# Expert weights in two halves with separate release, two of the four early pairs behind the rows' write, and row turns moved next to the raw turns

## What is computed

```python
def _L0_ffn_ref(x, Wg, bg, Wge, bge, W1, b1, W2, b2):
    G, E = (4, 8); KG, KE = (2, 2); D, M = (192, 768)
    xf = x.reshape(-1, D)
    comb = _combine_weights(xf, Wg, bg, Wge, bge)      # two groups of four, two experts in each: 4 of 32
    h = gelu(einsum('nd,edm->nem', xf, W1) + b1, approximate=False)
    y = einsum('nem,emd->ned', h, W2) + b2
    return einsum('ne,ned->nd', comb, y).reshape(x.shape)

h = tokens(x)                                   # (8, 64, 192)
h = h + _L0_attn_ref(_layernorm(h), ...)        # the first attention
h = h + _L0_ffn_ref(_layernorm(h), ...)         # the 32 experts
h = h + _L1_attn_ref(_layernorm(h), ...)        # the second attention
h = h + _L1_ffn_ref(_layernorm(h), ...)
```

## Time and profile before

| | us |
|---|---|
| median of 3 runs | 325.53 |
| the three runs | 325.77, 325.53, 323.02 |
| the profiled execution | 324.14 |
| its span, first to last instruction | 322.3 |
| PE busy | 290.0 |
| DVE busy | 152.6 |
| ACT busy | 112.4 |
| POOL busy | 64.6 |

### The profile page before, as it was taken

One profiled execution on the slowest core, in us unless ns is written; L12 is line 12 of the kernel. 1 busy time (PEld: TensorE's weight loads), 2 busy tenths in 40 slices (PEclk: granted clock), 3 DMA queues, 4 the chain that ended last, 5 costly groups with the idle time before them and its releaser, 6 DMA issues.

```text
span 322.3 us, 7312 instructions
## 1 busy us (share of the span) xinstructions
PE 290.0 (90%) x2642; PEld 194.5 (60%) x2642; DVE 152.6 (47%) x431; ACT 112.4 (35%) x386; POOL 64.6 (20%) x76
## 2 busy tenths in 40 slices
PE   7899699798999999998999999995689899969994
PEld 6858687573666565554565565553657687445553
DVE  0664335736365354434444542320159566554554
ACT  1256015203234535434435435434034464511110
POOL 4500000050223334333333233112034000000000
PEclk9999659959799999999999999999599999999999
DMA  7999402010299999999999999903840000000001
GB/s 276 395 421 420 176 2 65 1 47 13 53 411 418 407 411 416 416 413 421 411 416 417 412 414 415 395 26 126 321 206 1 4 2 2 0 0 0 0 2 49
DMA packets 13044, 70.91 MB, mean 220 GB/s; under 512 B 2849, under 2 KB 4070, under 8 KB 6736
## 3 DMA queue, kind: packets, MB, share of 16 engines
q1 hardware_dynamic: 10416, 65.62, 50.5%
q0 software_dynamic: 2304, 3.68, 3.4%
q10 hardware_dynamic: 288, 1.13, 0.9%
HBM read 68.97 MB, written 3.28 MB: 224 GB/s over the span
## 4 chain that ended last, share of the span: by engine, by line
PE 64%; DMA 19%; DVE 9%; issue 3%; ACT 2%; SPq 2%; DVEq 0%; ACTq 0%; POOLq 0%
PE ps L975 11%; PE ps L928 7%; DMA late_in<-in_experts 7%; PE ps L747 4%; DMA expert_w<-in_experts 4%; PE ps L933 4%; DMA probs<-in_experts 4%; PE ps L1050 4%; PE ps L1038 4%; PE ps L947 3%; PE ps L669 3%; DMA attn_rows<-in_attn_rows 2%; PE ps L1005 2%; PE ps L1041 2%; PE ps L918 2%
## 5 line engine op out<-in xcount | busy, mean ns | idle before, releaser
L637 ACT ACTIVATE turned<-ps,route_in 128x64 f32<-128x64 f32 x288 | 61.4, 340 | 83.4 <-PE ps L947 83.4
L484 POOL DMA_INDIRECT x_rows<-xn_rows,row_ids x24 | 24.9, 1038 | 117.5 <-DVE row_ids L1245 116.6
L1259 DVE COPY probs<-ps 128x768 f32<-128x768 f32 x24 | 23.0, 957 | 40.9 <-PE ps L933 40.9
L496 POOL DMA_INDIRECT y_picks<-fexp,row_ids x24 | 24.9, 1038 | 40.8 <-DVE fexp L1344 40.8
L975 PE MATMUL ps<-expert_w,turned 128*64 128x192 f32 x288 | 27.7, 345 | 0.0
L975 PE MATMUL ps<-late_in,turned 128*64 128x192 f32 x216 | 26.2, 331 | 1.2 <-ACT turned L637 1.2
L1344 DVE COPY fexp<-ps 128x192 f32<-128x192 f32 x24 | 8.6, 357 | 31.7 <-PE ps L975 31.7
L975 PEld LDWEIGHTS ps<-expert_w,turned 128*64 128x64 f32 x288 | 20.6, 143 | 4.6 <-issue 1.8
L975 PEld LDWEIGHTS ps<-late_in,turned 128*64 128x64 f32 x216 | 19.1, 137 | 6.3 <-ACT turned L637 2.4
L947 PE MATMUL ps<-cst,probs 128*128 128x128 f32 x144 | 21.1, 281 | 0.9 <-DVE probs L1259 0.9
L928 PE MATMUL ps<-expert_w,fexp 128*64 128x384 f32 x96 | 18.1, 498 | 2.8 <-DMA expert_w<-in_experts 2.0
(11 more groups left out here) (240 smaller groups left out, 460.1 us busy)
## 6 DMA issues: line engine op xcount, KB each, us to landing
expert_w<-in_experts SPq DMA_DIRECT2D x24, 1152.0 KB, 10.5
late_in<-in_experts SPq DMA_DIRECT2D x18, 1152.0 KB, 9.0
probs<-in_experts SPq DMA_DIRECT2D x6, 1152.0 KB, 11.5
late_in<-in_ffn_in SPq DMA_DIRECT2D x1, 2592.0 KB, 12.7
probsT<-in_patches SPq DMA_DIRECT2D x4, 384.0 KB, 7.0
qk_padT<-y_picks SPq DMA_DIRECT2D x4, 384.0 KB, 4.7
late_in<-in_attn_in SPq DMA_DIRECT2D x1, 864.0 KB, 4.3
attn_w<-in_attn_w SPq DMA_DIRECT2D x1, 673.5 KB, 9.0
```

The source lines that it names most:

```text
L484: pool.indirect_dma_start(out=x_rows[:, x_u, :], out_offset=None, in_=xn_rows, in_offset=bass.IndirectOffsetOnAxis(ap=row_ids[:, u % STEPS ...
L496: pool.indirect_dma_start(out=y_picks, out_offset=bass.IndirectOffsetOnAxis(ap=row_ids[:, u, 1:2], axis=0), in_=y_rows[:, u % RING, :], in ...
L637: last = act.activation(hidden[:, u % 2, half * (KH // 2) + c, slots_of(q)], ps[:, 4 + half, c * P + q * SLOTS:c * P + (q + 1) * SLOTS], A ...
L1259: dve.tensor_copy(raw.rearrange("p (h n) -> p h n", h=2), ps[:, 2:4, 0:HID // 2]).then_inc(raw_sb, 1)
```

## The change

Four things change.

1. Each expert comes in two transfers, W1 (columns 0 to 1151) and W2 (the rest), each with a semaphore of its own for each slot (`w1_dma`, `w2_dma`). The up matmuls wait for the first, the down matmuls for the second. The W1 half of pair `u + 5` is loaded when the up matmuls of pass `u + 1` are done, the W2 half of pair `u + 4` when the down matmuls of pass `u` are.
2. Of the four early pairs, 0 and 1 are loaded where they were, and 2 and 3 behind the write of `xn_rows`.
3. The row turns are done for `u + 3` behind the raw turns, at the end of the loop body, and VectorE copies them out behind the output copy. The 14 matmuls that make tables for the later passes go behind the first down matmuls.
4. Of the five fillers of 256 columns ahead of pass 0 one is left.

The diff, cut to its core:

```diff
-            def load_pair(i, ov_round, u):
+            def load_pair(i, ov_round, u, cols, done):
                 for q in range(PAIR):
                     e = expert_of(sp, i, ov_round, u, q)
-                    sp.dma_start(weights[u % RING * PAIR + q], dram["experts"][bass.ds(e, 1), :, :].rearrange("a p n -> (a p) n")).then_inc(w_dma[u % RING], 16)
-
-            for u in range(RING):
-                load_pair(0, None, u)
+                    sp.dma_start(weights[u % RING * PAIR + q][:, cols], dram["experts"][bass.ds(e, 1), :, cols].rearrange("a p n -> (a p) n")).then_inc(done[u % RING], 16)
+            def load_first(i, ov_round, u):
+                load_pair(i, ov_round, u, slice(0, W1_COLS), w1_dma)
+            def load_second(i, ov_round, u):
+                load_pair(i, ov_round, u, slice(W1_COLS, W_COLS), w2_dma)
+            for u in range(RING // 2):
+                load_first(0, None, u)
+                load_second(0, None, u)
             sp.wait_ge(xn_ready, 2 * NT)
             ...
+            for u in range(RING // 2, RING):
+                load_first(0, None, u)
+                load_second(0, None, u)
+            sp.wait_ge(up_mm, 1)
+            load_first(0, None, RING)
             def feed(i, ov_round, first, tiles):
                 for u in range(STEPS):
                     with where_tile(sp, tiles, ov_round, u):
+                        with where_tile(sp, tiles, ov_round, u + 1 + RING):
+                            sp.wait_ge(up_mm, i * STEPS + u + 2)
+                            load_first(i, ov_round, u + 1 + RING)
                         with where_tile(sp, tiles, ov_round, u + RING):
                             sp.wait_ge(down_mm, i * STEPS + u + 1)
-                            load_pair(i, ov_round, u + RING)
+                            load_second(i, ov_round, u + RING)
...
# TensorE, ids_in
+                if not (isinstance(tile, int) and tile < IDS_AHEAD):
+                    pe.wait_ge(rowsT_sb, tile - 1)
# TensorE, up_in
-                pe.wait_ge(w_dma[u % RING], 16 * PAIR * (i * (STEPS // RING) + u // RING + 1))
+                pe.wait_ge(w1_dma[u % RING], 16 * PAIR * (i * (STEPS // RING) + u // RING + 1))
# TensorE, experts
-                        with where_tile(pe, tiles, ov_round, u + 2):
-                            rows_in(i, u + 2)
...
+                        pe.wait_ge(w2_dma[u % RING], 16 * PAIR * (i * (STEPS // RING) + u // RING + 1))
...
                         with where_tile(pe, tiles, ov_round, u + 1):
                             turn_raw(i, u + 1, first)
+                        with where_tile(pe, tiles, ov_round, u + 3):
+                            rows_in(i, u + 3)
# TensorE, ahead of pass 0
-            keep_busy(5, 5)
+            keep_busy(1, 5)
...
             turn_raw(0, 0)
+            rows_in(0, 2)
# VectorE, results
-                        with where_tile(dve, tiles, ov_round, u + 2):
-                            dve.wait_ge(rowsT_mm, i * STEPS + u + 3)
-                            with where_tile(dve, tiles, ov_round, u + IDS_AHEAD):
-                                ids_out(i, u + IDS_AHEAD, first)
-                            rows_out(u)
+                        with where_tile(dve, tiles, ov_round, u + IDS_AHEAD):
+                            ids_out(i, u + IDS_AHEAD, first)
...
                         dve.tensor_copy(y_rows[:, u % RING, :], ps[:, 6 + u % 2, 0:D]).then_inc(y_ready, 1)
+                        with where_tile(dve, tiles, ov_round, u + 3):
+                            dve.wait_ge(rowsT_mm, i * STEPS + u + 4)
+                            rows_out(u + 3)
```

More of the change, by code:

```diff
@@ L348, in vit_tower @@
         pick_diag_ready, picks_mm = sem("pick_diag_ready"), sem("picks_mm")
-        w_dma, x_dma, y_dma = ([sem(f"{n}{u}") for u in range(RING)] for n in ("w_dma", "x_dma", "y_dma"))
+        w1_dma, w2_dma, x_dma, y_dma = ([sem(f"{n}{u}") for u in range(RING)] for n in ("w1_dma", "w2_dma", "x_dma", "y_dma"))
         rowsT_mm, rowsT_sb, up_mm, raw_sb, rawT_mm, gelu_done, down_mm, y_ready = (
@@ L957, in experts @@
                             ids_in(i, u + IDS_AHEAD, ov_round)
-                        with where_tile(pe, tiles, ov_round, u + 2):
-                            rows_in(i, u + 2)
                         if first and u == 0:
                             pe.wait_ge(ov_onehot_ready, 1)
-                            for c in range(KH):
-                                nc.tensor.matmul(ps[:, 7, 256 + c * NOV:256 + (c + 1) * NOV], b1_rows[:, c * P:(c + 1) * P], ov_onehot[:, :], start=True, stop=True)
-                            nc.tensor.matmul(ps[0:1, 7, 256 + KH * NOV:256 + (KH + 1) * NOV], const("row", NE), ov_onehot[:, :], start=True, stop=True).then_inc(ov_mm, 1)
                         if first and u == 1:
@@ L977, in experts @@
                         last.then_inc(down_mm, 1)
+                        if first and u == 0:
+                            for c in range(KH):
+                                nc.tensor.matmul(ps[:, 7, 256 + c * NOV:256 + (c + 1) * NOV], b1_rows[:, c * P:(c + 1) * P], ov_onehot[:, :], start=True, stop=True)
+                            nc.tensor.matmul(ps[0:1, 7, 256 + KH * NOV:256 + (KH + 1) * NOV], const("row", NE), ov_onehot[:, :], start=True, stop=True).then_inc(ov_mm, 1)
                         with where_tile(pe, tiles, ov_round, u + 1):
                             turn_raw(i, u + 1, first)
+                        with where_tile(pe, tiles, ov_round, u + 3):
+                            rows_in(i, u + 3)
             pe.wait_ge(tables_ready, 2)
@@ L1283, in _ @@
                                      op0=ALU.is_lt, op1=ALU.mult).then_inc(ov_onehot_ready, 1)
+            dve.wait_ge(rowsT_mm, 3)
+            rows_out(2)
             def ov_places():
```

## The result

| | before | after |
|---|---|---|
| median of the runs | 325.65 (323.02 to 328.97, 4 runs) | 309.04 (308.32 to 311.46, 4 runs) |
| the profiled execution, its span | 324.14, 322.3 | 308.32, 306.5 |
| mean granted clock | 0.951 | 0.953 |

A forecast was written before the change was run, and what follows sets the result against it. Bounds: a stall and half clock in the first attention, fillers before the passes, TensorE and then weights in them. Terms of -1.9, -3.0, -3.0, -1.1 and 0 took 324.14 to 315.1 us, 316.5 as a median; range 310.5 to 322.

The forecast's parts named there:

- A: First attention: early pairs 2 and 3 behind the rows' write remove TensorE's stall; -1.9 us, bounds 0 and 2.43.
- B: First attention, behind the stall: the half clock on the matmuls goes; -3.0 us, bounds 0 and 5.1.
- C: Expert passes: split pairs, W1 released by the up matmuls, end waits for weights; -3.0 us, bounds 0 and 3.0.
- D: Expert passes: row turns next to the raw turns cost 0.10 us less a pass; -1.1 us, at most 2.2.
- Rival 1: First attention: the stall stays, and the half clock with it; 321.4 us, chance 0.28.
- E: Start of the passes: four fillers fewer, earlier row turns against a possible half clock; 0 us, bounds -1.7 and +2.3.
- rival 3: Expert passes: row turns wait for gathers in a ring through VectorE; slower, up to 329.5 us, chance 0.04.
- Rival 2: Expert passes: split transfers bring nothing, weights stay 6.05 us a pass; 319.5 us, chance 0.14.
- Rival 4: Late passes: VectorE's wait for row turns loses the lead on weights; about 1 us, no chance of its own.

## Why the prediction was wrong

The direction held and each mechanism is there, but the sum was 7.6 us short by the medians. Against the profiled execution it was 6.8 short (15.8 for 9.0): 3.6 of it in A and B, 3.1 in C and D, 2.0 at the start of the passes, and 1.9 the other way at the end. Two steps failed. B, the largest shortfall, was sized at 3.0 for a half clock that costs 5.2 to 5.6 us, above even its bound of 5.1. C and D were costed one by one, C against a wrong length of the pass, and they are worth more together. By its steps:

**A, the stall (forecast -1.9).** Held. The issue piece of 2.16 to 2.43 us is in all six profiles with four pairs at the front, and is at most 0.79 long in the seven others that have no pause put in. The kernel with one pair behind the write shows that it takes load in that very stretch. In the writes' column, a stall without a dip costs 47.9 - 45.2 = 2.8 us (47.87 and 48.01, against the mean of the six profiles with at most 0.23 of stall), somewhat more than the piece and than my bound of 2.43. Rival 1, the stall as a matter of the instructions alone, is out. That the stalled engine was short of instructions can be read off the DMA view. Every profile has one instruction transfer of 16 KB shortly ahead of this place: it starts at 32.29 to 33.01 us in the six with four pairs at the front (in that of before, the transfer of the earlier trace rows, at 32.42), and at 29.58 to 31.22 in the eight others. After, in 29 to 31 us:

```profile
q8 instruction: 1, 0.02, 3.0%
```

In all nine profiles in which TensorE stands still behind the 117th small matmul, it goes on 2.35 to 2.73 us after the start of this transfer, also in the three with a short stall (0.22 us, transfer at 31.19; 0.23, at 30.54; 0.79, at 31.22). In the five in which the transfer starts 2.8 us or more ahead of the end of that matmul, there is no stall. The transfer itself takes 1.07 to 1.08 us under load and 0.93 to 1.33 without: what the load delays is its start. The Trainium skill, "Runtime: NRT & Kernel Launch" (Instruction fetch mechanics), has the fetch mostly hidden by the running block; these traces agree while the DMA engines rest, but for the 0.79 us, and show it bare at 410 GB/s.

**B, the half clock (forecast -3.0 of at most 5.1).** A failed step, mis-sized. With a dip the write leaves at 51.86 to 53.70, without one, behind the same stall, at 47.9: 5.2 us on the mean, 5.6 in this pair of traces. I took 3.0 because the dip might only come later. It did not: the stretch stays at 1.00 to its end. The bound of 5.1 was short because it began at the weighing: the 27 small matmuls ahead of it take 1.11 us at half clock before, and 0.68 in the kernel with one filler, which has the stall and no dip. A and B together are -8.51 for -4.9. What I had not seen is that the dip is a matter of chance. In the profiles it comes behind four of the six stalls and never without one, and the pause alone gives two groups of runs. That points to idleness of TensorE as what opens the way to it, and not to load, since in the pause the DMA engines move 4 GB/s; a trace of the slower group would be needed to show it. It fits with the spread: all runs of the kernel before lie from 316.28 to 329.44 us, and the fastest have the highest mean clock (0.977 at 316.28 and 316.63, 0.935 to 0.955 for those above 323), while the four runs of after spread over 3.1. From the fastest of before to the fastest of after (308.32) it is 8.0 us. So, as an estimate from these two, about half of the 16.6 is that the change takes away a bad chance.

**The start of the passes (forecast 0 for E and for the moved pairs).** -1.98, of which 1.5 lie ahead of the first up matmul and 0.5 behind it. The half clock at the first down matmuls is not there (2.00 for 3.78 us), and the one over the first row turns and up matmuls takes most of that back (0.66 and 2.67 for 0.23 and 1.51). The fillers are 1.2 of it in the changed kernel (32.68 to 31.50) and -0.2 in the one before, inside the bounds of E. The moved pairs cost nothing here, as forecast: with them at the front this stretch is longer, not shorter. Which edit removes the dip of the first down can't be said: both profiles of the kernel before have it (3.78 us in the first), and none of the five kernels with a single part does.

**C, the split releases (forecast -3.0, its upper end).** The other failed step. The sum kept "the pass costs 5.81 throughout", the mean from pass 4 to 9, and laid 211.91 against it. Two of those five passes carry work that comes once, the turning of the routing weights, and take 5.91 and 5.92; the others take 5.74. With split pairs in the old order each pass from 9 to 21 takes 5.74 and the last two 5.51, as there are no row numbers left to make: 79.92 / 14 = 5.71 for the 5.81. Weights had hidden that. C is worth 84.43 - 79.92 = -4.5 in the old order. And it had been costed as if D left it alone: in the new order, whole pairs against split is 124.63 against 117.79 over passes 2 to 23, -6.8.

**D, the row turns (forecast -1.1 of at most 2.2).** Mis-sized, and tied to C. I counted 0.10 us a pass for the turns. They save 0.15, and the down matmuls, now right behind the row numbers, save another 0.10 that no term had (2.10 to 2.00; in the last passes, which have no row numbers, they are at 2.10 again). Over 21 passes 0.22 to 0.25 is 4.6 to 5.3. Shown is 120.44 - 117.79 = -2.65 with split pairs, the rest being lost mainly in three late passes (rival 3), and 124.96 to 124.87 or 124.63, next to nothing, without. A shorter TensorE pass is worth nothing while the pass is 6.05 us of weights, and weights that are no bound are worth the more the shorter the pass is. By the marks over passes 2 to 23, C alone is worth 4.52 and D alone 0.09, together they are 7.17, so 2.6 us come of the two together. By the medians the single edits on the kernel before add to 7.9 + 4.1 + 0.6 + 1.2 = 13.8 us and not to 16.6; the last two of them are not resolved, and by the ratios the four add to some 9 us, so the medians alone would not show it.

**Rival 3, the ring through VectorE.** It came in small at most. From up of pass 16, 18 and 20 to the next it is 6.45, 6.00 and 6.33 us for 5.49, 2.3 us in all. Little of that is a wait for a gather: TensorE's idle time there is put down to a gather for 0.3 us, to VectorE's copy of the turned rows for 0.6, and to nothing that the profile shows for 0.4. With the marks late no gather is on the chain there, and 1.8 of the 2.3 us stay. So what lengthens these three passes is open. My argument against the rival fell all the same: landing should have gone to 4.5 us with rows of 4608 B. The DMA view over 76 to 196 us, after:

```profile
expert_w<-in_experts SPq DMA_DIRECT2D x34, 576.0 KB, 12.5
...
x_rows<-xn_rows,row_ids POOLq DMA_INDIRECT x19, 6.1
```

6.1 us is what whole rows gave. The Trainium skill's "DMA: Bandwidth & Descriptors" (Queues, rings and completion order) describes turns between the queues packet by packet. That a gather's row then waits for one row of weights was my reading of it, and these runs don't bear that out: halving the rows of weights left the landing where it was. What sets the 6.1 is open. The same page asks for at least 1 MiB a DMA for full bandwidth (Rules for kernel authors). Going below it cost some 2%: the halves of 576 KB run at 401 to 410 GB/s in the slices of the passes, whole ones at 407 to 421, and TensorE waited for no half.

**The end.** +1.86, outside all terms. Here too there are two sizes. Eleven of the twelve profiles taken in the experiments have 111.8 to 113.2 us there, the kernel before among them (112.1), and one has 110.3; the 110.39 of the first profile was the rarer case, so this is no cost of the change. What makes the difference was not looked into.

Rival 2, that C brings nothing, is out by the column of passes 9 to 23 above. Rival 4, VectorE's wait for the row turns as a loss of a microsecond, was not tested by itself.

## What to carry to other kernels

Look at what the DMA engines do in the few microseconds in which an engine runs its densest code: a load that nobody needs for 40 us cost 2.8 us there and, in four of six profiles, 5 us of clock behind it. Where two bounds lie within a few per cent of each other (5.7 to 5.8 of TensorE and 6.05 of weights), cost the edits together, since either alone runs into the other bound. Take the length of a pass from the passes without one-time work, not from a mean over all. A long transfer on the chain is not a long wait: look up how long the engine itself stood still. Where the kernel before has a spread of 8 us or more and its profile shows a dip behind a pause, the spread is itself a row to argue from.

## What the hardware showed unexpectedly

- Behind a pause of TensorE of some 2 us, the clock of the light matmuls goes from 2.4 to 1.2 GHz in some executions of the same program and not in others: behind 4 of 6 stalls of 2.16 to 2.43 us, and, read from times and mean clocks alone, in 8 of 10 runs with a pause put in while the DMA engines rest.
- Instruction supply shows once the DMA engines are full: 2.16 to 2.43 us amid 144 small matmuls at 410 GB/s, nothing to 0.79 us with them at rest. TensorE goes on 2.35 to 2.73 us after the instruction transfer starts, and it is that start which comes up to 3 us later under load, not the transfer that gets longer.
- Order alone changed the price of the same matmuls: two row turns 0.37 us behind the small matmuls of the row numbers, 0.22 behind the raw turns, and 24 down matmuls 2.10 us behind row turns, 2.00 behind the small matmuls of the row numbers.
- A gather under load lands after 6.1 us in the median beside rows of 9216 B and beside rows of 4608 B alike, and after 2.8 with nothing else moving.
